# Block places in registers: two per load instead of sixteen, in the block stage of a four-layer graph network

## Chip, cores and metric

The kernel runs on one core of a Trainium2 chip. The metric is the device time of one execution in microseconds (us); the figure given is the median of several runs.

## What is computed

Four graph layers on 1250 nodes with 512 features and 40000 edges, each followed by a residual and a layer norm. The changed stage prepares for the sums over edges (`segment_sum`) of the first three layers, of which two are shown:

```
def _L0_gnn_ref(x, edge_index, W1, b1, W2, b2):
...
    agg = jax.ops.segment_sum(x[src], dst, num_segments=N_NODES)
    h = (1.0 + eps) * x + agg
    h = jax.nn.relu(h @ W1 + b1)
    out = h @ W2 + b2
...
def _L2_gnn_ref(X, W, bias, edge_weight, edge_src, edge_dst):
...
    h = jnp.matmul(X, W)
    msgs = h[edge_src] * edge_weight[:, None]
    agg = jax.ops.segment_sum(msgs, edge_dst, num_segments=X.shape[0])
    return jax.nn.relu(agg + bias)
```

The second layer takes the mean over a node's neighbours, twice. The fourth builds a message per edge from its attributes and sums them by `dst`; it gathers rows by itself and is not part of the change.

## The kernel before

The first three layers do not gather rows per edge. The kernel builds two dense matrices over pairs of nodes once: how many edges lead from one node to another, and the sum of their weights. They lie side by side in the SBUF tile `adj_t`, seen as `adj` with an outer index of two. The edge sums are then products with them on PE (`agg_T`, line 643).

Up to about 388 us the edges are sorted into 416 chunks (`PAIR_CHUNKS`) of up to 128 edges, such that all edges of a chunk belong to one 128 x 128 block of the matrices. Where the block of each chunk lies in `adj_t`, a column number, is worked out too and stands in `pair_offs`, a row of integers in the SBUF tile `ybuf`. The sorted records come back from DRAM in one transfer (`dense<-pair_table`), and then the **block stage** begins, the one that the change touches. For each chunk:

- VectorE makes two one-hot matrices of 128 x 128 from the edges' row and column numbers: `select`, lines 1405 and 1406, the *selections*. The second counts up `sel_ready`.
- ScalarE (`sel_w`, lines 1045 and 1046) copies one to float32 and scales the other by the edges' weights, and counts up `selw_ready`.
- PE (`blocks`, lines 790 and 791) multiplies them: a bf16 product for the counts and a float32 one for the weights, both into one PSUM bank of eight, and counts up `blk_done`.
- VectorE adds the bank's 128 x 256 to the chunk's block of `adj_t`: line 1419, the *addition*. Its address isn't known when the kernel is built, so it comes from a register. It waits for `blk_done` and for the addition before it (`blk_added`, the wait of line 1417), since two chunks in a row can belong to one block.

VectorE runs this in the order of `turn`: for each place of a turn first the addition of chunk n, then the selections of chunk n + 8. So PE and ScalarE work up to eight chunks ahead of the additions. At the head of a turn (line 1410) one instruction, `TENSOR_LOAD`, reads the 16 block columns of the turn (`PLACES`) from `pair_offs` into sixteen registers. `turn(0)` and the last turn are written out, and those between are one hardware loop (line 1426) of 24 rounds, in which chunk numbers are register values: columns and semaphore counts are computed by small register instructions between the operations.

```
for c in range(2 * AB):
    select(c, c)
turn(0)
with dve.Fori(1, PAIR_CHUNKS // PLACES - 1) as i:
    turn(i)
turn(PAIR_CHUNKS // PLACES - 1, tail=True)
```

In the profile, VectorE's data operations appear as DVE, and what its sequencer does by itself (register work, loads into registers, branches) as DVEq. After the last addition (`blk_added` at 416) VectorE sums the matrix for the node degrees, PE starts the first product over it (`l0_agg`, line 643), SyncE loads `x` again, and GpSimd (POOL) begins its second round of scatters (`stage`, line 535, then 542), all at once.

Of the kernel before, what the change touches and what calls it, by code (L numbers as in the profile page):

```python
# [8 lines left out]
P = 128  # L9
# [11 lines left out]
AB = 4  # L21
# [68 lines left out]
AW_COLS = (NT - 1) * N + NT * P  # L90
# [14 lines left out]
def build(nc, x, src, dst, edge_attr_20, edge_attr_3, edge_weight,  # L105
# [4 lines left out]
    ds = bass.ds  # L110
# [9 lines left out]
    with ctx:  # L120
# [9 lines left out]
        adj = adj_t[:, :].rearrange("p (k n) -> p k n", k=2)  # L130
# [28 lines left out]
        pair_offs = ybuf[0:1, 0:4 * P].bitcast(i32)  # L159
# [209 lines left out]
        place = [(name, k) for name, count in STAGES for k in range(count)]  # L369
# [4 lines left out]
        PAIR_SCATTERED = 16 * len(DMA_COLS) // 2  # L374
        SRC_STEPS = EJ // STAGED
        AB_IT = PAIR_CHUNKS // (2 * AB)
        PLACES = 4 * AB
        assert PAIR_CHUNKS % PLACES == 0
        L3_LOADS = 8 + 2 * PRODUCTS

        block = ctx.enter_context(nc.Block())
# [824 lines left out]
        def _(dve):  # L1206
# [94 lines left out]
            def loop_block(t):  # L1301
                r, c0 = rows_of(t), t * N + t * P
                return adj[0:r, 0, c0:c0 + r], ident[0:r, 0:r]
# [39 lines left out]
            for k in range(1, 3):  # L1343
                link(v.tensor_tensor(pos_f, xyz_k[k], xyz_k[k], ALU.mult))
                last = v.tensor_tensor(tmp_f, tmp_f, pos_f, ALU.add)
# [57 lines left out]
            def select(n, c):  # L1403
                col = n * PAIR_COLS + PAIR_AT
                v.tensor_scalar(sel_b[:, c, 0, :], iotab[:, :], dense[:, ds(col, 1)], None, ALU.is_equal)  # L1405
                v.tensor_scalar(sel_b[:, c, 1, :], iotab[:, :], dense[:, ds(col + 1, 1)], None, ALU.is_equal).then_inc(sel_ready, 1)  # L1406

            def turn(i, tail=False):
                n0 = i * PLACES
                _, block_at = nc.values_load_multi_w_load_instructions(  # L1410
                    pair_offs[0:1, ds(n0, PLACES)], engines=[mybir.EngineType.DVE], min_val=0, max_val=AW_COLS - P,
                    skip_runtime_bounds_check_because="a sum of some of the steps between blocks; all of them make the last block's place")
                for k in range(PLACES):
                    c, n = k % (2 * AB), n0 + k
                    dve.wait_ge(blk_done, n + 1)
                    if not (isinstance(n, int) and n == 0):
                        dve.wait_ge(blk_added, n)
                    a = adj[:, :, ds(block_at[k], P)]
                    v.tensor_tensor(a, a, bank[c][:, 0:2 * P].rearrange("p (k n) -> p k n", k=2), ALU.add).then_inc(blk_added, 1)  # L1419
                    if not tail or k < PLACES - 2 * AB:  # L1420
                        select(n + 2 * AB, c)
# [9 lines that stand above are left out]
# [75 lines left out]
            for t in range(NT):  # L1506
                a, i = loop_block(t)
                last = v.tensor_tensor(a, a, i, ALU.subtract)
# [196 lines left out]
```

## Time and profile before

| | us |
|---|---|
| median of 3 runs | 2292.26 (2291.78 to 2292.79) |
| the profiled execution: its time | 2292.02 |
| the profiled execution: its span | 2290.2 |
| busy in the span: PE, VectorE, ScalarE, GpSimd | 2044.4, 1572.7, 1133.8, 1250.3 |
| granted TensorE clock, mean over the span | 0.935 |

The span is what the trace covers; the time of the same execution is 1.8 us longer. Busy times of different engines overlap, so they don't add up to the span. Register, branch, semaphore and load instructions of the sequencers are in none of them. Operations of VectorE that follow each other closely overlap by a few tenths of a microsecond in the records, so their durations add up to more than the time that they take.

### The profile page before, as it was taken

Reading aid. Unit: us, or ns where it says so; the run is one execution under the profiler, and the core shown is the slowest. Engines: PE = TensorE matmul, PEld = TensorE weight load, DVE = VectorE, ACT = ScalarE, POOL = GpSimd, SP = SyncE. Lnnn points to the kernel's source line nnn. Section 1 sums busy time; section 2 is a strip of 40 time slices with the busy share of each in tenths; the row PEclk is TensorE's granted clock in tenths of the full one; section 3 lists DMA queues with packets and bytes.
Section 4 is the critical chain, followed back from the end, with each engine's and each line's share of the span. In section 5 each row is a group of like instructions: output and inputs, shape, how many; then the busy total and the mean of one; then the engine's idle time right before and its main releaser. Section 6 shows DMA issues by size and latency. Waiting matters only on the chain.

```text
span 2290.2 us, 37213 instructions
## 1 busy us (share of the span) xinstructions
PE 2044.4 (89%) x7761; PEld 1150.3 (50%) x7761; DVE 1572.7 (69%) x4534; ACT 1133.8 (50%) x3234; POOL 1250.3 (55%) x1510
## 2 busy tenths in 40 slices
PE   3787794777878999999999799999999999999986
PEld 3443443555554555455444555555555555555545
DVE  8987666888885160111403588888888888888885
ACT  0476454777871010000010366666666666666654
POOL 1477885000005888888884356666666666666530
PEclk9698897787779999999999899999999999999998
DMA  5410320000002121121120233333333333333321
GB/s 194 158 14 3 88 69 17 0 0 0 0 0 64 39 43 21 21 61 21 19 64 12 77 97 98 97 97 97 99 100 99 100 97 97 98 98 101 93 67 46
DMA packets 75078, 147.00 MB, mean 64 GB/s; under 512 B 26829, under 2 KB 37570, under 8 KB 74631
## 3 DMA queue, kind: packets, MB, share of 16 engines
q0 software_dynamic: 44704, 95.66, 17.0%
q1 hardware_dynamic: 27356, 45.20, 5.9%
q10 hardware_dynamic: 2946, 5.28, 0.6%
q8 instruction: 33, 0.54, 0.1%
q14 instruction: 39, 0.32, 0.0%
HBM read 123.11 MB, written 22.40 MB: 64 GB/s over the span
## 4 chain that ended last, share of the span: by engine, by line
PE 64%; DVE 13%; POOL 10%; issue 8%; DVEq 3%; DMA 2%; ACT 0%; ACTq 0%; SPq 0%; POOLq 0%
PE ps L900 24%; PE ps L643 11%; POOL pair_table L528 10%; PE ps L662 8%; PE ps L838 4%; PE ps L883 3%; PE ps L885 3%; PE ps L884 3%; PE ps L886 3%; DVE adj_t L1419 3%; DVE dense L1405 2%; DVE adj_t L1219 1%; DVE dense L1406 1%; DMA pair_table<-dense 1%; DVEq L1405 1%
## 5 line engine op out<-in xcount | busy, mean ns | idle before, releaser
L900 PE MATMUL ps<-adj_t 128*128 128x512 f32 x1288 | 615.1, 599 | 14.4 <-DVE adj_t L1627 14.4
L1111 ACT ACTIVATE adj_t<-adj_t 128x128 f32<-128x128 f32 x966 | 315.4, 389 | 210.9 <-DVE adj_t L1606 209.8
L584 POOL DMA_INDIRECT adj_t<-z_table,adj_t x322 | 309.6, 961 | 154.2 <-DVE adj_t L1616 68.3
L900 PEld LDWEIGHTS ps<-adj_t 128*128 128x128 f32 x1288 | 231.5, 189 | 249.8 <-issue 214.0
L528 POOL DMA_INDIRECT pair_table<-dense x192 | 235.7, 1227 | 130.6 <-issue 119.7
L542 POOL DMA_INDIRECT src_table<-st_two,src_rows x216 | 261.3, 1210 | 70.4 <-issue 65.2
L791 PE MATMUL ps<-dense 128*128 128x128 f32 x832 | 223.3, 379 | 0.0
L662 PE MATMUL ps<-wring,dense 128*128 128x512 f32 (+1 forms) x480 | 210.0, 600 | 4.6 <-issue 3.2
L535 POOL DMA_DIRECT2D st_two<-records x54 | 31.9, 591 | 322.1 <-DVE adj_t L1419 321.9
L883 PE MATMUL ps<-dense_r 128*128 128x512 f32 x322 | 200.2, 622 | 2.3 <-POOL dense_r L592 2.3
L1419 DVE TENSOR_TENSOR adj_t<-adj_t,ps 128x256 f32 x416 | 170.9, 411 | 36.1 <-PE ps L791 34.4
L592 POOL TENSOR_TENSOR dense_r<-adj_t,dense_r 128x512 fp32r<-128x512 f32 x81 | 104.4, 1289 | 166.3 <-ACT dense_r L1120 166.2
L790 PE MATMUL ps<-dense 128*128 128x128 bf16 x416 | 106.7, 257 | 91.0 <-ACT dense L1046 71.9
L1608 DVE TENSOR_TENSOR adj_t<-adj_t,ps 128x384 f32<-128x384 f32 x322 | 175.6, 545 | 0.0
L643 PE MATMUL ps<-adj_t,xa 128*128 128x512 f32 (+1 forms) x480 | 170.3, 517 | 3.2 <-DVE adj_t L1419 3.2
L791 PEld LDWEIGHTS ps<-dense 128*128 128x128 f32 x832 | 170.1, 254 | 0.5
L1045 ACT ACTIVATE dense<-dense 128x128 f32<-128x128 bf16 x416 | 128.5, 309 | 81.6 <-DVE dense L1406 60.9
L1046 ACT ACTIVATE dense<-dense 128x128 f32<-128x128 bf16 x416 | 160.4, 386 | 0.0
L1627 DVE TENSOR_TENSOR adj_t<-adj_t,ps 128x1024 f32 x93 | 113.5, 1221 | 62.4 <-PE ps L900 61.4
L1606 DVE TENSOR_TENSOR adj_t<-adj_t,ps 128x256 f32<-128x256 f32 x322 | 133.2, 414 | 30.8 <-PE ps L886 27.0
L662 PEld LDWEIGHTS ps<-wring,dense 128*128 128x128 f32 (+1 forms) x480 | 90.8, 190 | 121.6 <-issue 121.6
L734 PE MATMUL ps<-dense 125*128 125x416 bf16 x640 | 141.0, 364 | 11.0 <-ACT dense L1021 9.3
(274 smaller groups left out, 3770.0 us busy)
## 6 DMA issues: line engine op xcount, KB each, us to landing
src_table<-dense SPq DMA_DIRECT2D x8, 656.0 KB, 6.6
adj_t<-z_table,adj_t POOLq DMA_INDIRECT x322, 3.4
records<-dense SPq DMA_DIRECT2D x1, 5000.0 KB
adj_t<-src_table SPq DMA_DIRECT2D x73, 64.0 KB
adj_t<-zeros SPq DMA_DIRECT2D x1, 4576.0 KB
src_table<-st_two,src_rows POOLq DMA_INDIRECT x216
st_two<-records POOLq DMA_DIRECT2D x54, 62.5 KB
adj_t<-zeros SPq DMA_DIRECT2D x1, 3328.0 KB
```

Source lines behind the costliest of these rows:

```text
L528: g.indirect_dma_start(out=pair_table, out_offset=bass.IndirectOffsetOnAxis(ap=rows_i[PAIR][0:EP, j:j + 1].bitcast(u32), axis=0), in_=pair ...
L542: g.indirect_dma_start(out=src_table, out_offset=bass.IndirectOffsetOnAxis(ap=rows_i[SRC][0:EP, j:j + 1].bitcast(u32), axis=0), in_=st_rec ...
L584: g.indirect_dma_start(out=zg[:, s, c, :], out_offset=None, in_=z_table, in_offset=bass.IndirectOffsetOnAxis(ap=dsti[:, s, c:c + 1].bitcas ...
L643: last = mm(b[:, 0:w], feats[:, t, m * P:(m + 1) * P], adj[:, k_of, t * N + c0:t * N + c0 + w], start=t == 0, stop=t == NT - 1)
L662: last = mm(b[0:r, :], lhs[:, k, t * P:t * P + r], w[:, k, :], start=a == 0 and k == 0, stop=a == len(parts) - 1 and k == KT - 1)
L791: mm(bank[c][:, P:2 * P], sel_f[:, c, 0, :], sel_f[:, c, 1, :], start=True, stop=True).then_inc(blk_done, 1)
L883: mm(bW[c], h_hi[:, s, e], wf2_hi, start=True, stop=False)
L900: last = mm(bank[6 + h], oh[:, c, :], msg[:, c, h * D:(h + 1) * D], start=c == c0, stop=c == c0 + count - 1)
L1046: A(sel_f[:, c, 1, :], sel_b[:, c, 1, :], ACT.Copy, scale=dense[:, ds(n * PAIR_COLS + (PAIR_AT + 2), 1)]).then_inc(selw_ready, 1)
L1111: last = A(msg[:, c, (2 + k) * P:(3 + k) * P], msg[:, c, MSG:MSG + P], ACT.Copy, scale=side[:, s, c, C_Y - ATT + k:C_Y - ATT + k + 1])
L1419: v.tensor_tensor(a, a, bank[c][:, 0:2 * P].rearrange("p (k n) -> p k n", k=2), ALU.add).then_inc(blk_added, 1)
L1608: v.tensor_tensor(msg[:, c, 5 * P:8 * P].rearrange("p (a n) -> p a n", a=3), zg[:, s, c, P:4 * P].rearrange("p (a n) -> p a n", a=3), b[:, ...
```

## The change

`PLACES`, the chunks of a turn, becomes 8 instead of 16, and the load into registers moves from the head of the turn into the loop over its places, at every even place, where it reads two block columns. Lines after it are one further down in the new kernel: the addition is line 1420, the load line 1413, the loop line 1427.

```
-        PLACES = 4 * AB
+        PLACES = 2 * AB
...
             def turn(i, tail=False):
                 n0 = i * PLACES
-                _, block_at = nc.values_load_multi_w_load_instructions(
-                    pair_offs[0:1, ds(n0, PLACES)], engines=[mybir.EngineType.DVE], min_val=0, max_val=AW_COLS - P,
-                    skip_runtime_bounds_check_because="a sum of some of the steps between blocks; all of them make the last block's place")
                 for k in range(PLACES):
                     c, n = k % (2 * AB), n0 + k
+                    if k % 2 == 0:
+                        _, block_at = nc.values_load_multi_w_load_instructions(
+                            pair_offs[0:1, ds(n, 2)], engines=[mybir.EngineType.DVE], min_val=0, max_val=AW_COLS - P,
+                            skip_runtime_bounds_check_because="a sum of some of the steps between blocks; all of them make the last block's place")
                     dve.wait_ge(blk_done, n + 1)
                     if not (isinstance(n, int) and n == 0):
                         dve.wait_ge(blk_added, n)
-                    a = adj[:, :, ds(block_at[k], P)]
+                    a = adj[:, :, ds(block_at[k % 2], P)]
```

What VectorE's queue holds at the head of the loop and inside a turn, before. `ISA` and `REGISTER_ALU` are register instructions, those of line 1419 carry the waits for the addition:

```order
L1426 UNCONDITIONAL_BRANCH
L1426 ISA
L1410 TENSOR_LOAD ybuf
L1415 REGISTER_ALU
L1419 ISA [waits blk_added,blk_done]
L1419 TENSOR_TENSOR adj_t<-adj_t,ps 128x2x128
L1405 ISA
L1405 TENSOR_SCALAR dense<-iotab,dense 128x128
L1406 ISA
L1406 TENSOR_SCALAR dense<-iotab,dense 128x128
L1415 REGISTER_ALU
L1419 ISA [waits blk_added,blk_done]
```

The same queue after the change, from the second place of a turn on to the third:

```order
L1416 REGISTER_ALU
L1420 ISA [waits blk_added,blk_done]
L1420 TENSOR_TENSOR adj_t<-adj_t,ps 128x2x128
L1405 ISA
L1405 TENSOR_SCALAR dense<-iotab,dense 128x128
L1406 ISA
L1406 TENSOR_SCALAR dense<-iotab,dense 128x128
L1413 ISA
L1413 TENSOR_LOAD ybuf
L1416 REGISTER_ALU
L1420 ISA [waits blk_added,blk_done]
```

Between the second selection and the register instruction of the next addition there now stand an address instruction and a load; the head of the loop keeps its load. A loop turn holds four loads and eight additions instead of one load and sixteen additions.

The last turn, written out, has no selections after the change:

```order
L1413 TENSOR_LOAD ybuf
L1420 ISA [waits blk_added,blk_done]
L1420 TENSOR_TENSOR adj_t<-adj_t,ps 128x2x128
L1420 ISA [waits blk_added,blk_done]
L1420 TENSOR_TENSOR adj_t<-adj_t,ps 128x2x128
L1413 TENSOR_LOAD ybuf
```

Before, its first eight places still had them. The queues of PE, ScalarE, GpSimd and SyncE hold what they held.

## Rows read from the trace of the kernel before

**Rows 1.** The page, the chain that ended last: shares of the span by engine.

```profile
PE 64%; DVE 13%; POOL 10%; issue 8%; DVEq 3%; DMA 2%; ACT 0%; ACTq 0%; SPq 0%; POOLq 0%
```

**Rows 2.** Busy time by stretch: the block stage and the first us behind it.

```profile
core 0: us, PE busy (x) PEld busy (x) DVE busy (x) ACT busy (x) POOL busy (x), PEclk, DMA share, GB/s
388.00:701.00 313.00, 238.87 (x1249) 172.96 (x1250) 276.75 (x1249) 248.69 (x832) 0.00 (x0) 0.78 0.00 0
700.00:705.00 5.00, 4.21 (x6) 1.91 (x7) 4.70 (x5) 0.00 (x0) 1.19 (x2) 0.54 0.55 174
```

**Rows 3.** The table of waits: who waited for whom, us in total, times, longest.

```profile
POOL st_two L535 <- DVE adj_t L1419: 321.9, 1, 321.9
...
DVE adj_t L1419 <- PE ps L791: 34.4, 25, 1.5
```

**Rows 4.** VectorE's timeline, one loop turn into the next: start, us, what, [idle before <-releaser].

```profile
419.77 0.41 DVE L1419 TENSOR_TENSOR adj_t<-adj_t,ps 128x256 f32 x1
...
424.37 0.41 DVE L1419 TENSOR_TENSOR adj_t<-adj_t,ps 128x256 f32 x1
...
424.86 0.24 DVE L1406 TENSOR_SCALAR dense<-iotab,dense 128x128 bf16<-128x128 bf16 x1
426.52 0.42 DVE L1419 TENSOR_TENSOR adj_t<-adj_t,ps 128x256 f32 x1 [1.41 <-PE ps L791]
...
427.20 0.42 DVE L1419 TENSOR_TENSOR adj_t<-adj_t,ps 128x256 f32 x1
```

**Rows 5.** The chain in order of time, the block stage: start, us, what.

```profile
413.08 1.11 DVEq L1410
...
677.36 1.10 DVEq L1410
```

**Rows 6.** The same chain seen close, around the load at 425.13.

```profile
424.64 0.04 DVEq L1426
...
425.13 1.10 DVEq L1410
426.23 0.03 issue
...
426.52 0.10 DVE adj_t L1419
...
427.38 0.07 DVEq L1406
```

**Rows 7.** The first load by itself, and VectorE's timeline beside it.

```profile
L1410 DVEq TENSOR_LOAD <-ybuf x1: 1362/1362/1362, 388.7 to 388.7; - x1
...
388.77 0.25 DVE L1406 TENSOR_SCALAR dense<-iotab,dense 128x128 bf16<-128x128 bf16 x1
...
389.42 0.25 DVE L1406 TENSOR_SCALAR dense<-iotab,dense 128x128 bf16<-128x128 bf16 x1
...
390.07 0.24 DVE L1406 TENSOR_SCALAR dense<-iotab,dense 128x128 bf16<-128x128 bf16 x1
```

**Rows 8.** Sequencer instructions by line: ns min/median/max, first and last start.

```profile
L1410 DVEq TENSOR_LOAD <-ybuf x26: 1098/1102/1362, 388.7 to 689.1; - x26
L1620 DVEq TENSOR_LOAD <-src_offs x93: 297/305/329, 1324.2 to 2235.3; - x93
L1426 DVEq FUSED_REGOPS  x24: 74/74/80, 400.5 to 677.2; - x24
```

**Rows 9.** VectorE's timeline: the load between the loop and the last turn, then the last additions.

```profile
688.62 0.41 DVE L1419 TENSOR_TENSOR adj_t<-adj_t,ps 128x256 f32 x1
...
690.38 0.42 DVE L1419 TENSOR_TENSOR adj_t<-adj_t,ps 128x256 f32 x1 [1.02 <-PE ps L791]
...
700.32 0.42 DVE L1419 TENSOR_TENSOR adj_t<-adj_t,ps 128x256 f32 x1 [0.20 <-DVE adj_t L1419]
```

## Prediction

> **What bounds the kernel now.** I read the chain that ended last first [rows 1]. Over the whole span it lies mostly on PE, so a reader has to ask about the block stage by itself. That stage runs from about 388 to 701 us: PE is busy for 239 of 313 us there, ScalarE for 249, VectorE for 277 [rows 2], and POOL waits for the last VectorE addition before it may begin its next transfers [rows 3]. Everything later follows that addition, by POOL directly and by PE through the first product over the finished matrix, so what the stage gains or loses arrives whole at the end.
>
> Next, what sets the pace in the stage. Seven chunks separate the additions at 419.77 and 424.37 [rows 4], so a chunk costs 4.60 / 7 = 0.657 us. The three VectorE operations of a chunk follow each other without a gap; that is VectorE's own rate. After sixteen chunks the chain shows a register load of 1.10 us. The loads at 413.08 and 677.36 are 22 turns apart [rows 5]: (677.36 - 413.08) / 22 = 12.01 us a turn, of which 16 x 0.657 = 10.51 is chunks. **The load with the loop's jump costs 1.50 us a turn.** The waits table puts this idle time down to PE [rows 3], but the chain's close view has the load itself on it [rows 6], and selections run eight chunks ahead of the additions, so PE has some 5 us of lead. I believe the chain.
>
> What matters for the change is which part of VectorE a load occupies. The first load started at 388.7 and took 1.36 us, and VectorE's operations went on through it, at 388.77, at 389.42 and at 390.07 [rows 7]: there ten queued selections were ahead. So a load does not stop the engine, it stops its sequencer, the part that does register work, waits and hands operations over. A load is free as far as the sequencer is ahead. In the steady stage it hardly is. With the addition at 424.37, the sequencer has handed over both selections of that chunk and reaches the next instruction at 424.64 (+0.04) [rows 6]. There it meets the wait for the addition itself, which ends at 424.37 + 0.41 = 424.78. It idles for only 0.1 us per chunk. After a load ends, the next addition starts 426.52 - 426.23 = 0.29 us later, for a register sum, two waits and their register work [rows 6].
>
> **The change, part by part.** Instead of 26 loads of sixteen places there are 416 / 2 = 208 loads of two. Of these, 50 loop turns hold 3 each inside a turn (150) and 49 more follow the jump from one turn to the next; one is at the loop's entry, one at the exit, one at the very start, and 3 + 3 stand in the first and last turns, which are written out.
>
> *Price of a load.* Sixteen values take 1.10 us, one value 0.305 (93 loads later in the program, while VectorE works) [rows 8]. On a line between them each value adds (1.10 - 0.305) / 15 = 0.053, so two take **0.36 us**. Bounds: 0.305 (the one-value load), and 0.36 x 1.36 / 1.10 = 0.45 if work beside it slows it as the first load was slowed [rows 7, 8]. I take 0.36, since the one-value loads already ran beside work.
>
> *A load inside a turn.* The sequencer arrives 424.64 - 424.37 = 0.27 us after the addition's start. New there is register work for the address, 0.08 by the similar instruction at the loop's head plus 0.04 to the next [rows 6, 8]. The load then takes 0.36 and the way to the next addition 0.29: 0.27 + 0.12 + 0.36 + 0.29 = 1.04 us from addition to addition in place of 0.657, so +0.38. The wait for the previous addition (0.41 long) is over by then and costs nothing. One thing is added from the chunk after a stall: its addition comes 0.68 after the first one, not 0.657 [rows 4], and the sequencer has done the second selection's register work at 427.38 + 0.07, 0.25 after the addition at 427.20, where the steady chunk would give about 0.20 (424.64 less the step of 0.07, against 424.37) [rows 4, 6]. Together 0.07, so **+0.45 us each; 150 x 0.45 = 67.5 us**. Below: 0.38 - 0.05 = 0.33 (one-value load, no lateness), 49.5 us.
>
> *Turn boundaries.* Each now carries a load 1.10 - 0.36 = 0.74 shorter, but again 0.05 of lateness: 1.50 - 0.74 + 0.05 = 0.81. 49 x 0.81 = 39.7 us, where 23 x 1.50 = 34.5 stood before: **+5.2 us**. So twice as many jumps use up everything that the shorter loads give back.
>
> *Entry, exit and ends.* The entry and exit loads (exit: 690.38 - 688.62 = 1.76 from addition to addition [rows 9]) each become 0.74 shorter: **-1.5 us**. The first load lies beside queued selections. In the written-out turns no register work stands around the operations, and in the last one there are no selections, so its 0.36 us fits beside an addition of 0.42 that has to be waited for anyway [rows 9]. I cost these six at nothing; if that cover failed they would be 6 x 0.38 = 2 us. Eight chunks that pass from the written-out ends into the loop keep their rate.
>
> *Beside it.* PE and ScalarE get more idle time in the stage and wait for VectorE, as now. No DMA is issued or moved past another: SP and POOL only start their next work later by the sum. PE's granted clock averages 0.78 in the stage and 0.54 just after it, then 1.00 [rows 2]; a thinner stage might leave the lower of its two levels (1.2 GHz against 2.4) standing a little longer, worth at most the 5 us of that stretch, and I take none.
>
> A rule to weigh: the one-value load here takes 0.305 us [rows 8]. The Trainium skill (DMA: Bandwidth & Descriptors, the section on latency and other measured facts) gives a floor of about 600 ns for a register load, which the 93 loads of this trace contradict. By it the sum would come out some 50 us higher; that is a rival below.
>
> **Sum:** 67.5 + 5.2 - 1.5 = +71.2. On the profiled execution: its span 2290.2 becomes 2361.4, its time 2292.0 becomes 2363.2. The median of the runs is 0.2 higher than that execution, so 2363.5, rounded to **2363 us** (+3.1%).
>
> **The rivals.**
> *1. The loads are covered, and the jumps decide.* If the sequencer did run ahead far enough, the 150 loads inside turns would cost nothing. Then 49 x 0.81 - 34.5 - 1.5 = +3.7 us: 2296, no change. If a boundary load were covered as well, a boundary would shrink by 0.36 + 0.04 to 0.41: 20.1 - 34.5 - 2.3 = -17 us, **2275, faster**. For it speaks the first load, which cost nothing. Against it speaks the idle time of 0.1 us per chunk; full cover of the in-turn loads needs 0.36 + 0.12 = 0.48. This mechanism decides for faster only from the point where the sequencer idles for that long in every second chunk. Chance: 0.03 for 2296, 0.04 for 2275.
> *2. A load has a high fixed price.* If the two-value load took not 0.36 but 0.60, 199 loads on the path would add 199 x 0.24 = 48 us: **2411**. What speaks for it is only that no two-value load is in the trace; one-value and sixteen-value loads on both sides of it speak against. It is the figure of the Trainium skill's page named above. Chance 0.05.
> *3. The lower forecast.* The same mechanism with the one-value price and no lateness: 49.5 + 49 x 0.71 - 34.5 - 1.6 = +48, **2340**. It is within my forecast and not counted apart.
> That the change does not do what it says is ruled out by the order of VectorE's instructions, which has a load before every second addition and the loop's end after eight.
>
> **How the numbers follow.** My forecast (each in-turn load partly covered, the rest on VectorE's path) has 0.88. Its own span is 2340 (above) to 2381 (0.09 more for each of 199 loads, +18). I widen to 2332, for an address instruction that costs only half of its 0.12 in the low case (-9), and to 2390, for 5 us of clock and a few us unaccounted; 2275, 2296 and 2411 stay outside, which leaves out 0.12 and some tail. A difference under about 0.2% (4.6 us) cannot be told from none here. Faster 0.04, the same 0.03, slower 0.93.
>
> **What would show it right.** In the profile after: 208 register loads on VectorE's sequencer of about 0.36 us; additions 1.09 and 0.68 us apart by turns (1.04 plus 0.05 of lateness, 0.657 plus 0.02) and 1.45 across the jump; a loop turn of eight chunks of about 7.4 us; the last addition ending near 772 instead of 701, with everything after it unchanged in length. It would be wrong if the loads were 0.6 us, if additions stayed 0.657 apart across a load (then the sequencer is further ahead than I read), or if the stretch after the last addition changed by more than 5 us.

## The result and the profile after

| | before | after |
|---|---|---|
| median of 5 runs, us | 2292.26 (2291.78 to 2292.79) | 2386.4 (2383.25 to 2386.95) |
| ratio after / before | | 1.0408, interval 1.0394 to 1.0421 |
| span of the profiled execution, us | 2290.2 | 2384.6 |
| start of the last addition, us | 700.32 | 795.29 |
| from there to the end of the span, us | 1589.9 | 1589.3 |

The kernel became 94 us slower, where I had forecast 71 us. My range was 2332 to 2390 us; 2386.4 lies near its upper end. The whole loss lies ahead of the last addition; what follows it kept its length. The page of the changed kernel, the chain that ended last and the two groups that answer to POOL's wait [rows 3] and to the block stage's additions:

```profile
PE 62%; DVE 12%; issue 10%; POOL 9%; DVEq 5%; DMA 2%; ACT 1%; ACTq 0%; SPq 0%; POOLq 0%
...
L535 POOL DMA_DIRECT2D st_two<-records x54 | 32.0, 592 | 417.0 <-DVE adj_t L1420 416.7
L1420 DVE TENSOR_TENSOR adj_t<-adj_t,ps 128x256 f32 x416 | 174.2, 419 | 113.1 <-issue 99.9
```

POOL waits 416.7 us where it waited 321.9 [rows 3], 95 us longer. The idle time in front of the additions is now put down to "issue", that is to VectorE's own sequencer. The stage by itself and the 5 us behind it, busy time by engine, to be held against [rows 2]:

```profile
388.00:796.00 408.00, 305.01 (x1249) 218.69 (x1250) 294.78 (x1250) 248.83 (x832) 0.00 (x0) 0.51 0.00 0
795.00:800.00 5.00, 4.24 (x6) 1.94 (x7) 4.70 (x5) 0.00 (x0) 1.19 (x2) 0.54 0.57 183
```

PE shows 305 us of work for the same matmuls that took 239 [rows 2]: its granted clock fell from 0.78 to 0.51 of full speed, about the lower of its two levels, in a stage where VectorE now pauses after every second chunk. That stayed hidden: 305 us lie in 408. The 5 us behind the stage have the clock 0.54 as before.

The loads, by line:

```profile
L1413 DVEq TENSOR_LOAD <-ybuf x208: 521/535/783, 389.0 to 793.9; - x104
L1413 DVEq FUSED_REGOPS  x150: 53/53/53, 397.9 to 787.7; - x150
```

There are 208, as the change says. But one of two values takes **0.535 us**, not the 0.36 of my line between one and sixteen values [rows 8]. The timeline of one loop turn, its additions alone (the selections between them are left out):

```profile
420.94 0.42 DVE L1420 TENSOR_TENSOR adj_t<-adj_t,ps 128x256 f32 x1 [0.85 <-issue]
421.60 0.42 DVE L1420 TENSOR_TENSOR adj_t<-adj_t,ps 128x256 f32 x1
...
422.78 0.42 DVE L1420 TENSOR_TENSOR adj_t<-adj_t,ps 128x256 f32 x1 [0.44 <-issue]
423.44 0.41 DVE L1420 TENSOR_TENSOR adj_t<-adj_t,ps 128x256 f32 x1
...
424.65 0.42 DVE L1420 TENSOR_TENSOR adj_t<-adj_t,ps 128x256 f32 x1 [0.46 <-issue]
425.33 0.42 DVE L1420 TENSOR_TENSOR adj_t<-adj_t,ps 128x256 f32 x1
...
426.55 0.42 DVE L1420 TENSOR_TENSOR adj_t<-adj_t,ps 128x256 f32 x1 [0.47 <-issue]
427.22 0.42 DVE L1420 TENSOR_TENSOR adj_t<-adj_t,ps 128x256 f32 x1
...
428.81 0.42 DVE L1420 TENSOR_TENSOR adj_t<-adj_t,ps 128x256 f32 x1 [0.85 <-issue]
```

Across a load inside a turn the additions are 1.18 to 1.22 apart (421.60 to 422.78, and so on), without one 0.66 to 0.68, across the jump 1.59 (427.22 to 428.81). A turn of eight chunks takes 428.81 - 420.94 = 7.87 us. The chain close by, around the load of the second pair, shows each step of the path:

```profile
421.67 0.14 DVE adj_t L1420
421.81 0.07 issue
421.88 0.05 DVEq L1413
421.93 0.24 DVE dense L1405
422.18 0.16 DVEq L1413
422.34 0.18 issue
422.52 0.04 DVEq L1416
...
422.78 0.11 DVE adj_t L1420
```

The sequencer comes to the address instruction at 421.88, 0.28 after the addition at 421.60. The load takes 0.52 us by its own record, from 421.97 to 422.49 (the chain shows it in pieces, since the selections run beside it until 422.34), and the addition follows 0.29 later, just as before the change. VectorE has nothing left to do from 422.34 on.

### The profile page after: what moved, and what is told of

Same layout as the page of the kernel before. It is cut to its first block, busy times and chain, and to the rows that moved or that the text cites. A ratio compares the mean times of both kernels' runs of the same rounds, so it can differ in the third digit from the quotient of the medians.

```text
span 2384.6 us, 37837 instructions
## 1 busy us (share of the span) xinstructions
PE 2109.7 (88%) x7761; PEld 1196.4 (50%) x7761; DVE 1593.9 (67%) x4534; ACT 1134.1 (48%) x3234; POOL 1253.0 (53%) x1510
## 4 chain that ended last, share of the span: by engine, by line
PE 62%; DVE 12%; issue 10%; POOL 9%; DVEq 5%; DMA 2%; ACT 1%; ACTq 0%; SPq 0%; POOLq 0%
PE ps L900 23%; PE ps L643 11%; POOL pair_table L528 9%; PE ps L662 8%; PE ps L838 4%; PE ps L883 3%; PE ps L885 3%; PE ps L886 3%; PE ps L884 3%; DVE dense L1405 3%; DVEq L1413 2%; DVE adj_t L1420 2%; DVE adj_t L1219 1%; DMA pair_table<-dense 1%; DVE dense L1406 1%
## 5 line engine op out<-in xcount | busy, mean ns | idle before, releaser
L791 PE MATMUL ps<-dense 128*128 128x128 f32 x832 | 288.3, 470 | 0.0
L535 POOL DMA_DIRECT2D st_two<-records x54 | 32.0, 592 | 417.0 <-DVE adj_t L1420 416.7
L790 PE MATMUL ps<-dense 128*128 128x128 bf16 x416 | 119.0, 286 | 123.1 <-ACT dense L1046 122.8
L791 PEld LDWEIGHTS ps<-dense 128*128 128x128 f32 x832 | 215.8, 319 | 0.4
```

Of the source, the lines that this page charges most:

```text
L791: mm(bank[c][:, P:2 * P], sel_f[:, c, 0, :], sel_f[:, c, 1, :], start=True, stop=True).then_inc(blk_done, 1)
```

## The experiments

Two questions were open. Why does a load of two values cost 0.535? And what makes up the 94 us: the loads' own time, the doubled jumps, or the register work around them? Each experiment is the changed kernel with `turn` written for two numbers, `PLACES` (chunks in a turn) and `LOAD` (places per load): the load stands at `k % LOAD == 0`. With 8 and 2 it is the changed kernel; with 16 and 16 it is the kernel before. In all but 7 and 10 the lines stand one further down than in the changed kernel: the load is line 1414, the addition line 1421, PE's matmuls lines 791 and 792. Where more is changed, the experiment says so. Times are given as differences from the kernel before in the same job, whose median was 2288.7, 2290.3 and 2291.6 us in the three jobs. Those without an interval are one execution each; within a job the executions of the kernel before lie up to 4 us apart, so differences below that say nothing by themselves. The length of the stage, from the start of the first addition to that of the last, is given beside them: 309.8 us in the kernel before, 404.5 in the changed one.

### 1. Loads of two without the doubled jumps

```
+        PLACES = 16
+        LOAD = 2
```

> Loads of two as in the change, but turns of sixteen chunks as before, so no jump is added. Theory: 94.4 us of loss are the loads' own time on the sequencer (0.535 each, so 0.56 more per pair of chunks inside a turn, from the profile after) plus twice as many jumps. By it: 24 x (7 x 0.56 + 0.93) = 116, with the ends about 120, less the 37 of before: +83 us, 2375. Rival, that the shorter loop costs most (jump and refetch): the loss falls to about half, below 2340. Second rival, that jumps cost nothing: no less than 2384.

Measured: 2366.1, **+77 us**. Same 208 loads, median 0.528 us; the stage is 384.8 us long, against 404.5 in the changed kernel and 309.8 before. Both rivals fall: the shorter turns account for no more than 20 us of the 94, and the loads, with the register work around them, for the rest. +77 is 6 us less than the +83 expected. The timeline says why:

```profile
430.91 0.41 DVE L1421 TENSOR_TENSOR adj_t<-adj_t,ps 128x256 f32 x1
...
432.01 0.42 DVE L1421 TENSOR_TENSOR adj_t<-adj_t,ps 128x256 f32 x1 [0.36 <-issue]
...
435.17 0.42 DVE L1421 TENSOR_TENSOR adj_t<-adj_t,ps 128x256 f32 x1
...
436.35 0.42 DVE L1421 TENSOR_TENSOR adj_t<-adj_t,ps 128x256 f32 x1 [0.45 <-issue]
```

From the eighth place of a turn on, no register sum for the chunk number (`REGISTER_ALU`) stands in front of an addition, and the gap across a load is 1.10 (430.91 to 432.01) instead of 1.18 (435.17 to 436.35). One register instruction less is 0.08 us less, and 96 of the loads are followed by such an addition: 8 us. In the changed kernel every addition of the loop that follows a load has its sum. So the 20 us between the two kernels are not the 26 jumps alone. An estimate from the gaps: a jump adds 1.59 - 1.20 = 0.39 us to a load that stands there anyway, 10 us for 26 of them; the register sums are 8 us; and eight more loads stand in the written-out turns here, with 0.80 instead of 1.20 across each, 3 us.

### 2. Eight places per load

```
+        PLACES = 8
+        LOAD = 8
```

> Turns of eight chunks as in the change, but one load of eight at the head of each: the jumps are kept, the extra loads inside a turn go. Theory: each of 49 boundaries costs 0.93 - 0.535 + the load of eight. If price runs as a fixed part and a slope through two (0.535) and sixteen (1.10), 0.040 a value and 0.455 fixed, eight take 0.77: 49 x 1.17 + 3 - 37 = +23 us, 2315. If price runs straight from one value (0.305) to sixteen, eight take 0.68: +19 us. Rival, that jumps cost most of it: over 2340.

Measured: 2300.8, **+12 us**, with a stage of 322.2 us. The rival falls: the jumps alone do not cost most of it. Both of my prices were too high as well (0.77 and 0.68); the load of eight took 0.596.

### 3 and 4. One place and four places per load

```
+        PLACES = 16
+        LOAD = 1
```

> Turns of sixteen, one place per load, 416 loads. It asks why two values took 0.535 where my line from 0.305 (one) to 1.10 (sixteen) gave 0.36. Theory A, a load of one value is cheap by its count: its loads take 0.305, in-turn 0.33 each, 24 x 15 x 0.33 + 23 x 0.70 + 4 - 37 = +102 us, 2394. Theory B, all loads from this row have a fixed part of 0.455 and the later loads of 0.305 are cheap for another reason (where the row lies, what form): 0.495 each, about +173 us, 2465.

```
+        PLACES = 16
+        LOAD = 4
```

> Turns of sixteen, four places per load, 104 loads. Fixed part and slope (0.455 + 0.040 a value): 0.615 a load, 24 x 3 x 0.64 + 23 x 1.01 + 4 - 37 = +36 us, 2328. Straight line from one value: 0.464 a load, 24 x 3 x 0.49 + 23 x 0.86 + 4 - 37 = +22 us, 2314.

Measured: one per load 2379.9, **+91 us**, stage 399.2 us; four per load 2295.1, **+6 us**, stage 313.7 us. Theory B fell: a single value from this row is cheap too (theory A had +102). For four per load both expectations, +36 and +22, were far too high. The load lines of experiments 1, 2, 3 and 4, each its own kernel:

```profile
L1414 DVEq TENSOR_LOAD <-ybuf x208: 521/528/778, 389.8 to 775.1; - x104
```
```profile
L1414 DVEq TENSOR_LOAD <-ybuf x52: 594/596/855, 387.9 to 706.7; - x52
```
```profile
L1414 DVEq TENSOR_LOAD <-ybuf x416: 297/300/556, 389.0 to 789.5; - x139
```
```profile
L1414 DVEq TENSOR_LOAD <-ybuf x104: 339/344/609, 388.8 to 701.9; - x104
```

Two values 0.528, eight 0.596, one 0.300, **four 0.344**. Four values are cheaper than two. No line fits, but a new theory does: values come in groups of four, 0.344 for the first and 0.253 for each further one (0.344 + 0.253 = 0.597 for eight, 0.344 + 3 x 0.253 = 1.10 for sixteen), and a load of fewer than four goes value by value, 0.300 and 0.228 for the next.

### 5. Four read, two used

```
-                            pair_offs[0:1, ds(n, 2)], engines=[mybir.EngineType.DVE], min_val=0, max_val=AW_COLS - P,
+                            pair_offs[0:1, ds(n, 2 * LOAD)], engines=[mybir.EngineType.DVE], min_val=0, max_val=AW_COLS - P,
```

(This is the argument of the changed kernel's load; `PLACES` is 8 and `LOAD` is 2, so four columns are read.)

> The changed kernel with the same 208 loads in the same places, but each reads four columns and uses the first two. The four runs before gave a median of 0.300 us for one value, 0.528 for two, 0.344 for four, 0.597 for eight, 1.10 for sixteen. Theory (groups of four): a load reads whole groups of four at 0.344 for the first and 0.253 for each further one, and what is left over one by one, 0.300 and 0.228. By it every load here gets 0.184 shorter although it reads more: 199 x 0.184 = 37 us less than the changed kernel, and about 57 us more than the kernel before. Rival, that the price belongs to the places where the loads stand and not to their count: no difference from the changed kernel.

Measured: 2410.1, **+120 us**, 25 more than the changed kernel where 37 less was expected. A miss that showed what was lacking. Two loads of one turn, 2 us apart, by the load line alone:

```profile
L1414 DVEq TENSOR_LOAD <-ybuf x1: 964/964/964, 423.4 to 423.4; - x1
L1414 DVEq TENSOR_LOAD <-ybuf x1: 348/348/348, 425.7 to 425.7; - x1
```

The one that begins at column 2 of its turn takes 0.964, the one at column 4 takes 0.348, and so they alternate through the stage. 0.964 is about 0.300 + 3 x 0.22, four single values. The theory that follows, and that experiments 9 and 10 put to the test: a group of four has its low price only where it begins at a column that four divides.

### 6. Loads of two, all turns written out

```
-            turn(0)
-            with dve.Fori(1, PAIR_CHUNKS // PLACES - 1) as i:
+            for i in range(PAIR_CHUNKS // PLACES - 1):
                 turn(i)
```

with `PLACES` 16 and `LOAD` 2. Chunk numbers are constants then, so no jump, no address instruction and no register work around the selections is left.

> Turns of sixteen, loads of two, all turns written out: no jump, no register work for addresses and counts. Theory (the sequencer's path decides): a load starts 0.06 after the addition's start and ends at 0.59, the next addition follows at 0.80, so 0.15 per load, about 200 x 0.15 = 30 us, where the kernel before loses 37 in the stage: 7 us less than the kernel before. Rival, that fetching the long straight code costs more (one gap of 0.34 stood in the written-out last turn): some 10 to 40 us more than that.

Measured: 2289.5, **-1 us**, with the same 208 loads at 0.533. The stage is 307.2 us long against 384.8 in experiment 1, which differs in the loop alone. So 78 us hang on its jumps and its register work. The difference of 1 us from the kernel before is within the spread of that kernel's executions. The timeline:

```profile
420.52 0.41 DVE L1421 TENSOR_TENSOR adj_t<-adj_t,ps 128x256 f32 x1
...
421.68 0.42 DVE L1421 TENSOR_TENSOR adj_t<-adj_t,ps 128x256 f32 x1 [0.40 <-PE ps L792]
...
422.35 0.41 DVE L1421 TENSOR_TENSOR adj_t<-adj_t,ps 128x256 f32 x1
```

Most loads leave 0.80 between additions, as expected. The gap of 1.16 here (420.52 to 421.68) is one of thirteen of 0.97 to 1.18, together some 4 us. They go with fetches of the straight code: the page's instruction queue moves 55 packets in this kernel and 39 in the kernel before, in this order:

```profile
q14 instruction: 55, 0.45, 0.1%
q14 instruction: 39, 0.32, 0.0%
```

Between 404.5 and 692 us that is 16 packets of 8 KB, one every 17.2 us, against none before. By the trace's times each of the thirteen gaps ends between 0.2 us after the start of such a packet and 0.8 us before it. How the fetch holds the sequencer, no run here shows, and some packets have no gap beside them.

### 7. The price table that was not

Written-out turns with loads of sixteen, and a second load in 25 of them.

> All turns written out with loads of sixteen, and in 25 of them a second load whose values nothing uses, of 1 to 16 values from several start columns. Groups of four: 3 values 0.76, 5 values 0.57, 6 values 0.80, 7 values 1.03, 12 values 0.85, 15 values about 1.53 and so above sixteen (1.10). Rival, that only powers of two are read in one piece, or that the start column decides: 12 would be as 8 + 4 by either, but loads of four from column 1, 2 or 3 would cost like four single ones, 0.98.

Its trace holds 26 loads, not 51:

```profile
L1416 DVEq TENSOR_LOAD <-ybuf x26: 1096/1098/1366, 388.2 to 670.8; - x26
```

Those whose values nothing used are not there, and the question stayed open. What ran was the kernel before with its turns written out: 2271.0, **-19 us**, with a stage of 291.6 us. A load of sixteen (1.10) then adds 0.71 to the 0.657 from addition to addition, where it added 1.49 in the loop.

### 8. Loads of four, all turns written out

> Turns of sixteen, loads of four, all turns written out. Theory: a load starts 0.06 after the addition's start, takes 0.344 and is over at 0.40; the next addition could follow at 0.61, before VectorE has done its 0.657 of work. So all 104 loads are covered and the stage's whole loss of 37 us goes: 2252 where the kernel before has 2289 on this chip. Rival, cost of fetching straight code: between that and no gain.

Measured: 2255.5 (2255.0 to 2256.1), **-35 us**, ratio 0.9845 (0.9828 to 0.9861). This version is the fastest of all that were run. The expected figure was 2252. Its additions with the load line:

```profile
L1414 DVEq TENSOR_LOAD <-ybuf x104: 338/343/605, 388.6 to 663.0; - x104
```
```profile
L1421 DVE TENSOR_TENSOR adj_t<-adj_t,ps 128x256 f32 x416 | 169.3, 407 | 3.4 <-issue 2.0 <-DVE adj_t L1421 1.4
```

and the two additions on either side of the load that begins at 421.7:

```profile
421.63 0.41 DVE L1421 TENSOR_TENSOR adj_t<-adj_t,ps 128x256 f32 x1
...
422.28 0.40 DVE L1421 TENSOR_TENSOR adj_t<-adj_t,ps 128x256 f32 x1
```

104 loads of 0.343 run beside VectorE's operations and almost nothing is seen of them: 3.4 us of idle time in front of 416 additions, against 36.1 in the kernel before. The stage is 275.0 us long; 415 steps of 0.657 are 272.7, and nine gaps of 0.95 to 0.98, each just ahead of an instruction packet as in experiment 6, are the rest. PE is granted 0.96 of its full clock in this stage, where VectorE hardly pauses. Of the 35 us, 19 come with writing the turns out (experiment 7) and 16 more with loads of four in place of sixteen.

### 9. The same 208 loads, each of one aligned group

```
-                            pair_offs[0:1, ds(n, 2)], engines=[mybir.EngineType.DVE], min_val=0, max_val=AW_COLS - P,
+                            pair_offs[0:1, ds(n - k % 4, 4)], engines=[mybir.EngineType.DVE], min_val=0, max_val=AW_COLS - P,
...
-                    a = adj[:, :, ds(block_at[k % 2], P)]
+                    a = adj[:, :, ds(block_at[k % 4], P)]
```

> Mends the experiment before: its loads of four took 0.346 where they began at a column that four divides, and 0.965 where they began two further on. Here the changed kernel keeps its 208 loads in their places, but each reads the group of four that its two places lie in, from the group's first column, and uses the two. Theory (an aligned group of four is one read, all else goes value by value): every load takes 0.345 in place of 0.535, 199 x 0.19 = 38 us less than the changed kernel, so about 56 us more than the kernel before: what my prediction's price of 0.36 would have given. Rival, that the price hangs on the place in the program: loads at every second place stay at 0.53 or above.

Measured: 2339.0 (2337.5 to 2339.5), **+47 us**, ratio 1.0207 (1.0190 to 1.0224). Its lines of loads and of their address instructions, then its additions in one turn:

```profile
L1414 DVEq TENSOR_LOAD <-ybuf x208: 337/343/611, 389.7 to 747.2; - x104
L1414 DVEq FUSED_REGOPS  x50: 53/53/53, 399.6 to 740.0; - x50
```
```profile
420.44 0.41 DVE L1421 TENSOR_TENSOR adj_t<-adj_t,ps 128x256 f32 x1
421.45 0.42 DVE L1421 TENSOR_TENSOR adj_t<-adj_t,ps 128x256 f32 x1 [0.26 <-PE ps L792]
422.14 0.42 DVE L1421 TENSOR_TENSOR adj_t<-adj_t,ps 128x256 f32 x1
423.09 0.42 DVE L1421 TENSOR_TENSOR adj_t<-adj_t,ps 128x256 f32 x1 [0.20 <-issue]
423.75 0.41 DVE L1421 TENSOR_TENSOR adj_t<-adj_t,ps 128x256 f32 x1
425.14 0.42 DVE L1421 TENSOR_TENSOR adj_t<-adj_t,ps 128x256 f32 x1 [0.65 <-issue]
```

The loads' median is 0.343, in the same number and the same places, and each reads twice as much. The rival (a price by place) is out. The stage is 356.9 us long, 47.6 less than the changed kernel's. 199 x (0.535 - 0.343) = 38 of that is the loads. The rest has its line too: 50 address instructions instead of 150, since two loads of one group share an address. Where one remains the gap is 1.01 instead of 1.21 (420.44 to 421.45 against 423.44 to 424.65), 0.20 less, the load alone; where it is gone the gap is 0.95 instead of 1.22 (422.14 to 423.09 against 425.33 to 426.55 of the changed kernel), so 0.07 more; 100 x 0.07 to 0.09 is 7 to 9 us.

### 10. The price table, with values that are used

Written-out turns; each turn's sixteen places are read in pieces of uneven size, and all are used.

> All turns written out, and each turn's sixteen places read in pieces of uneven size, a pattern of eleven turns: 3+1+5+7, 6+2+8, 12+4, 2+8+6, 1+15, 1+4+4+4+3, 5+3+8, 16, 10+6, 2+4+10, 3+13. It gives the table of prices that the run with unused values did not (its extra loads were not in its trace). Theory (single values 0.300 then 0.225 each; an aligned group of four 0.344, or 0.253 as a further one): 3 from a group's start 0.75; 6 from one 0.79; 12 from one 0.85; 5 from one 0.57; 4 from the second column 0.98. Open is what 8 from the third column takes: 1.15 if it is read as 2 + 4 + 2, and 1.9 if a load that begins inside a group goes value by value to its end.

Measured: 2301.1, **+9.5 us**, and 72 loads. Some of their lines, one load each, in this order: twelve values from column 0, four from column 12, three from column 0, four from column 1, eight from column 2, fifteen from column 1:

```profile
L1419 DVEq TENSOR_LOAD <-ybuf x1: 850/850/850, 413.9 to 413.9; - x1
L1419 DVEq TENSOR_LOAD <-ybuf x1: 346/346/346, 422.3 to 422.3; - x1
L1419 DVEq TENSOR_LOAD <-ybuf x1: 765/765/765, 512.7 to 512.7; - x1
L1419 DVEq TENSOR_LOAD <-ybuf x1: 967/967/967, 452.5 to 452.5; - x1
L1419 DVEq TENSOR_LOAD <-ybuf x1: 1855/1855/1855, 426.4 to 426.4; - x1
L1419 DVEq TENSOR_LOAD <-ybuf x1: 3387/3387/3387, 438.7 to 438.7; - x1
```

The prices that the theory gave before the run came out within 0.05 us. The open point is settled on the dear side: a load that begins inside a group goes value by value to its end, also over the whole groups in it. Eight from column 2 cost 1.86, and fifteen from column 1 cost 3.39, three times a load of sixteen. Loads that begin at a group's first column read whole groups and then the remainder one by one: five 0.62, six 0.83, ten 1.09.

## Why the prediction was right in direction and short in size

**The mechanism held.** I had said that a load stops VectorE's sequencer and not its engine, that the sequencer has only about 0.1 us in hand per chunk, and that most of a load would therefore lie on the stage's path. The profile after shows exactly this path, and experiments 6 and 8 show it from the other side. With the register work gone the same loads of two cost 0.15 each, and loads of four next to nothing. So the first rival (loads covered) was a true mechanism for another kernel: it decides where the sequencer comes to the load early enough for the load's length.

**The term that was mis-sized is the price of a load.** "On a line between them each value adds 0.053, so two take 0.36 us" was wrong, and my upper bound of 0.45 too: 0.535. The two rows that I interpolated between were of different kinds. One value is read by itself, and sixteen from an aligned column come as four groups. Two values are on the first side, priced as two single ones. Between the rows there was no line but a step. With the measured price the sum gains (0.535 - 0.36) x 199 = 35 us, which makes 2398: outside my range.

**The other terms were 12 us too high together** and hid a third of that. In three in-turn pairs and one at the jump, a turn takes 7.87 us where I had 3 x 1.76 + 2.12 = 7.41. Had the load been at 0.36, the gap across it would have been 1.20 - 0.175 = 1.03, where I had 1.09 with the lateness. The address instruction took 0.05 and not 0.08, and the sequencer was late by 0.01 (0.28 after the addition, not 0.27) instead of 0.05. Per load that is 0.06 less, and 199 x 0.06 = 12. So 71 + 35 - 12 = 94. **That the time fell inside my range is thus luck in part**: the price was above the bound of 0.45 that I had given it, and only terms that erred the other way brought the sum back. Experiment 9 is the check: at 0.343 a load and 100 address instructions fewer it gives +47, thus +54 to +56 with them. That is 15 to 17 below my sum: the 12, and 199 x 0.017 = 3 for 0.343 in place of 0.36. (The six loads in the written-out ends, which I put at nothing, left 0.76 to 0.80 between additions where 0.62 to 0.66 is the pace, together about 1 us.)

**The rival with a high fixed price** (0.60 a load, 2411) was nearer in price than my own figure, and the change came out between the two. Yet its reason is wrong: there is no floor of 0.6. The Trainium skill (DMA: Bandwidth & Descriptors, "Latency and other measured facts") puts one at about 600 ns; the runs have 416 loads at 0.300 and 104 at 0.344. What is dear per value is a size or a start that breaks the groups of four.

**The boundaries.** I forecast that twice as many jumps would use up what the shorter loads give back (+5.2 us). With the load at 0.535 a boundary costs 2.25 - 1.31 = 0.94, and 49 of them 46 us against 34.5. Experiment 1 sets aside the 26 added jumps and is 20 us shorter in the stage, but about 10 of these are the jumps; the others are register sums and written-out places that went with them.

**Beside it.** Everything behind the last addition kept its length within 0.6 us, as forecast, and PE's lower clock in the stage was hidden. PE's lead was shorter than the 5 us that I gave it: in the trace before, the chunk selected at 424.86 was through PE at 426.30 (a matmul of line 791 from 425.86, 0.44 long), and its addition, eight chunks after 424.37, would be due at 429.63, 3.3 us later. The chain was right all the same: with the loads of four in experiment 8 the waits that the table had put down to PE are gone, though PE does the same matmuls.

## What to carry to other kernels

A load into registers occupies the sequencer, so its cost is its length less what the sequencer is ahead of its engine at that point; read that lead from the trace (here the wait for the last addition held it to 0.1 us) before cutting one load into many. Take a load's price from a row of the same size and the same start, not from a line between other sizes: here four aligned values (0.34) were cheaper than two (0.53). Of the sizes run with written-out turns (two, four and sixteen) four was best, the one that the cover could hide whole; eight was not run there. Where the sequencer is the bound, constants in place of register values help: inside the hardware loop no choice of load beat the sixteen of the kernel before, while writing the turns out gave 19 us with that same load and 35 us with loads of four.

## What the runs showed of the hardware that I had not expected

- **Loads into VectorE's registers have the price of groups of four 4-byte values, if they start at a column that four divides.** One value 0.300 us, two 0.53, three 0.76, four 0.344, five 0.62, six 0.83, eight 0.60, twelve 0.85, sixteen 1.10. From any other start each value is paid for alone, about 0.22 for each after the first: four 0.97, six 1.42, eight 1.86, fifteen 3.39. What a load does inside is in no trace; the prices are all that is shown, for one row of the SBUF tile `ybuf`.
- **PE's granted clock went with how steadily VectorE fed it**: 0.96 of full speed in the stage where VectorE hardly paused (experiment 8), 0.78 with a pause of 1.4 us every sixteen chunks (before), 0.51 with a pause of 0.4 us or more in every second chunk (after). PE's work for the same matmuls was 214, 239 and 305 us. The length of the stage does not decide it: experiment 6, 307.2 us long with its pauses spread over every second chunk, has 0.60 where the kernel before, 309.8 us long, has 0.78. The lower clock cost nothing in these stages, since PE was not the bound: experiment 6 has the lower clock and is the shorter of the two.
- **A register instruction of VectorE's sequencer costs 0.07 to 0.09 us of path**, though its own record says 0.04 to 0.05 (experiments 1 and 9). The rest is the step to the next instruction.
